# Two feed-forward blocks written as unrolled programs of units across group borders, and the store of the output by group

## What is computed

```
h = jax.nn.silu(hg) * hu              # hg = w_gate x, hu = w_up x, 16 experts
ye = einsum('bsei,edi->bsed', h, w_down)
y = einsum('bsed,bse->bsd', ye, combine) + silu(g) * u @ shared_down_w.T
```

## Time and profile before

| what | us |
|---|---|
| median of 3 runs (lowest to highest) | 5502.06 (5499.12 to 5502.11) |
| profiled execution, its time | 5501.84 |
| its span, first to last instruction | 5500.1 |
| busy in the span: PE / DVE / ACT / POOL | 4484.7 / 3591.8 / 2738.8 / 2465.6 |
| mean granted clock of TensorE, as a share of full speed | 0.897 |

### The profile page before, as it was taken

The page is one execution under the profiler, slowest core; times in us unless marked ns, Lnnn a source line. Parts: engine busy times, 40 slices in busy tenths (PEclk is TensorE's granted clock), DMA queues, the critical chain, the costliest instruction groups (busy, mean ns, idle before and its releaser), DMA issues. The chain is left out here.

```text
span 5500.1 us, 116174 instructions
## 1 busy us (share of the span) xinstructions
PE 4484.7 (82%) x45623; PEld 2775.8 (50%) x45624; DVE 3591.8 (65%) x6873; ACT 2738.8 (50%) x4638; POOL 2465.6 (45%) x2282
## 2 busy tenths in 40 slices
PE   7768999999999999678647888877887689967577
PEld 5545666666666666336523334343563444424344
DVE  4347777777777776475286999999553436547355
ACT  3325666666666666553225656655553235533121
POOL 8436666666666665250275666666332210001100
PEclk7789999999999999788668999999998779977788
DMA  1001111111111111000000000000000000020000
GB/s 23 16 29 28 45 37 29 49 33 45 36 43 37 29 37 29 5 0 3 12 1 14 0 1 1 0 1 1 15 1 0 13 9 16 1 70 5 20 1 8
DMA packets 110396, 102.35 MB, mean 19 GB/s; under 512 B 37095, under 2 KB 80375, under 8 KB 109111
## 3 DMA queue, kind: packets, MB, share of 16 engines
q1 hardware_dynamic: 107831, 94.14, 6.9%
q0 software_dynamic: 2048, 1.05, 0.1%
HBM read 40.18 MB, written 1.18 MB: 8 GB/s over the span
## 5 line engine op out<-in xcount | busy, mean ns | idle before, releaser
L4201 POOL TENSOR_TENSOR l_attn_read<-l_attn_state,l_attn_c_rows 128x1024 f32<-128x1024 f32 x256 | 604.4, 2362 | 291.6 <-DVE l_attn_state L4103 174.4
L2999 POOL TENSOR_TENSOR l_ffn_t<-l_ffn_t 128x512 f32<-128x512 f32 x384 | 487.3, 1269 | 506.5 <-DVE l_ffn_t L2866 506.5
L2597 PE MATMUL psum<-l_ffn_wq,l_ffn_xsT 128*128 128x512 f32 x1152 | 599.6, 612 | 99.3 <-DVE l_ffn_t L2866 97.8
L3823 PE MATMUL psum<-l_attn_read,ident 128*128 128x512 f32 x1024 | 489.9, 596 | 7.3 <-DVE l_attn_yz L4111 5.0
L3005 POOL TENSOR_TENSOR l_ffn_t<-l_ffn_t,l_ffn_ss 128x512 f32<-128x512 f32 x384 | 400.5, 1043 | 0.7 <-DVE l_ffn_ss L2881 0.7
L2862 DVE TENSOR_TENSOR l_ffn_t<-psum,l_ffn_tab 128x512 f32<-128x512 f32 x384 | 258.8, 674 | 121.3 <-ACT l_ffn_sq L2748 118.6
L4103 DVE TENSOR_TENSOR_SCAN l_attn_state<-l_attn_decay,psum 128x1024 f32<-128x1024 f32 x144 | 329.0, 2285 | 4.5
L2645 PEld LDWEIGHTS psum<-l_ffn_pT,l_ffn_v 64*64 64x64 f32 x3072 | 248.8, 135 | 142.9 <-issue 138.8
L2597 PEld LDWEIGHTS psum<-l_ffn_wq,l_ffn_xsT 128*128 128x128 f32 x1152 | 179.4, 191 | 274.0 <-DVE l_ffn_t L2866 237.9
L3979 ACT ACTIVATE l_attn_decay<-l_attn_dt,l_attn_a 128x1016 f32<-128x1016 f32 x256 | 292.9, 1144 | 37.2 <-DVE l_attn_state L4100 33.8
L2645 PE MATMUL psum<-l_ffn_pT,l_ffn_v 64*64 64x64 f32 (+1 forms) x3072 | 306.1, 227 | 1.2 <-ACT l_ffn_pT L2764 1.2
(11 more groups left out here) (908 smaller groups left out, 11415.5 us busy)
## 6 DMA issues: line engine op xcount, KB each, us to landing
l_ffn_vx<-l_ffn_v SPq DMA_DIRECT2D x192, 128.0 KB
l_ffn_vx<-l_ffn_v SPq DMA_DIRECT2D x384, 64.0 KB
l_ffn_wq<-in_L_ffn_Wqkv SPq DMA_DIRECT2D x6, 1536.0 KB, 6.3
l_xattn_toep<-s4d_taps SPq DMA_DIRECT2D x4, 2048.0 KB, 17.1
l_ffn_wo<-in_L_ffn_Wo SPq DMA_DIRECT2D x6, 512.0 KB, 4.1
l_ffn_w<-in_L_ffn_W SPq DMA_DIRECT2D x6, 341.0 KB
l_ffn_w<-in_L_ffn_w SPq DMA_DIRECT2D x3, 512.0 KB, 4.1
x_all<-in_x SPq DMA_DIRECT2D x4, 256.0 KB, 4.2
```

The source lines that it names most:

```text
L2597: nc.tensor.matmul(ring[it % 2], xsT[:, n % 2, m % G, :], w, start=True, stop=True).then_inc(itemed, 1)
L2999: nc.gpsimd.tensor_tensor(t1[:, m % G, i, :], t1[:, m % G, i, :], t2[:, x % 3, :], ALU.add).then_inc(added, 1)
L3823: last = nc.tensor.matmul(total[:, h * GT:(h + 1) * GT], K.ident[:], read[:, k % 3, h * GT:(h + 1) * GT], start=(n == 0), stop=(n == N - 1 ...
L4201: nc.gpsimd.tensor_tensor(read[:, k % 3, :].rearrange("p (h n) -> p h n", h=2), state[:, k % 3, :].rearrange("p (h n) -> p h n", h=2), row ...
```

## The change

Both blocks lose the device loop and the stages in it. Each is one stage with one unrolled program per engine over all NU units: in L2 a group is 2 shared units (a half of the shared expert each) and 8 experts, 40 units in all; in L3 one shared unit and 16 experts, 68 in all. In step s PE does `first(s)` and the later parts of the units s - 1 and s - 2, also where these belong to the group before. What prepares the next group (transposes of x, router, Exp or Tanh, routing steps) stands at fixed steps in the middle of a group; `sc`, `sel`, `total` and `xT` are doubled for it. x is transposed from `x_all` directly. The shared unit's addition starts `total` from x_all (the residual). The norm is `moments` on DVE (four bn_stats, four bn_aggr) behind the last addition of a group, then root and scaling on POOL, which writes x_all: in L2 POOL does it behind the scaling for expert 2 of the next group, in L3 it has nothing else. In L3, SP issues the three loads (sd first) and, when a group is normed, the store of that group, all inside the stage; the final store stage is gone. The matmuls, their shapes and their number are the same; a shared unit of L2 adds its half with its own DVE addition in place of accumulation in PSUM, and ACT's copy of the shared output is gone.

The parts of L2 that set the order (PE, ACT, DVE; `shared(n)` is true for the first two units of a group):

```diff
-        with nc.Fori(0, NB // G) as i:
-            b0 = i * G
-            load_group(K, b0)
...
+            def wait_x3_free(eng, n):
+                if shared(n):
+                    eng.wait_ge(product, n + 1)
+                else:
+                    eng.wait_ge(x3_ready, experts_to(n))
...
+                def first(n):
+                    if n >= 1:
+                        pe.wait_ge(h_ready, n)
+                        wait_x3_free(pe, n - 1)
...
+                    nc.tensor.matmul(H, by_h, src, start=True, stop=True).then_inc(h_dot, 1)
+                    nc.tensor.matmul(X3, by_x3, src, start=True, stop=True).then_inc(x3_dot, 1)
...
+                turn_x(0)
+                route(0)
+                for s in range(NU + 2):
+                    if s + 1 < NU and not shared(s + 1):
+                        turn(s + 1)
+                    if s < NU:
+                        first(s)
+                    if 1 <= s <= NU and not shared(s - 1):
+                        second(s - 1)
+                    if s >= 2:
+                        turn_back(s - 2)
+                    if s < NU and s % PER == 4 and group(s) + 1 < NG:
+                        turn_x(group(s) + 1)
+                    if s < NU and s % PER == 5 and group(s) + 1 < NG:
+                        route(group(s) + 1)
...
+                for s in range(NU):
+                    if s + 1 < NU and not shared(s + 1):
+                        move(s + 1)
+                    silu(s)
+                    if not shared(s):
+                        move_x3(s)
+                    if s % PER == 4 and group(s) + 1 < NG:
+                        move_x(group(s) + 1)
+                    if s % PER == 7 and group(s) + 1 < NG:
+                        exp(group(s) + 1)
...
+                for s in range(1, NU + 2):
+                    if s <= NU:
+                        multiply(s - 1)
+                    if s >= 2:
+                        add(s - 2)
+                        if (s - 2) % PER == PER - 1:
+                            moments(group(s - 2))
+                    if s < NU and s % PER == 6 and group(s) + 1 < NG:
+                        begin_route(group(s) + 1)
+                    if s < NU and s % PER == 8 and group(s) + 1 < NG:
+                        end_route(group(s) + 1)
```

`multiply(n)` waits for turn_back(n - 2) and, of a shared unit, for its Silu and X3; it writes `pr[n % 2]`. `add(n)` waits for turn_back(n). Of L3:

```diff
-        load(K, *[(w[i][:], I[pre + n].rearrange("e a b -> a e b")) for i, n in ((1, "w_up"), (2, "w_down"))], (sd[:], I[pre + "shared_down_w"]))
...
+            @block.sync
+            def _(sp):
+                sp.dma_start(sd[:], I[pre + "shared_down_w"]).then_inc(down_in, 16)
+                sp.dma_start(w[1][:], I[pre + "w_up"].rearrange("e a b -> a e b")).then_inc(up_in, 16)
+                sp.dma_start(w[2][:], I[pre + "w_down"].rearrange("e a b -> a e b")).then_inc(down_in, 16)
+                for g in range(NG):
+                    sp.wait_ge(normed, G * (g + 1))
+                    sp.dma_start(K.out[g * G:(g + 1) * G].rearrange("b t d -> t b d"), K.x_all[:, g * G:(g + 1) * G, :]).then_inc(written, 16)
+                sp.wait_ge(written, 16 * NG)
...
+                for s in range(NU + 2):
+                    if s < NU:
+                        first(s)
+                    if s >= 2:
+                        second(s - 2)
+                    if s < NU and s % PER == 5 and group(s) + 1 < NG:
+                        turn_x(group(s) + 1)
+                    if s < NU and s % PER == 7 and group(s) + 1 < NG:
+                        route(group(s) + 1)
...
+                for s in range(NU + 2):
+                    if s < NU:
+                        multiply(s)
+                    if s >= 2:
+                        add(s - 2)
+                        if (s - 2) % PER == PER - 1:
+                            moments(group(s - 2))
+                    if s < NU and 8 <= s % PER < 13 and group(s) + 1 < NG:
+                        route(group(s) + 1, s % PER - 8)
...
-                sp.dma_start(out.rearrange("b t d -> t b d"), K.x_all[:]).then_inc(stored, 16)
-                sp.wait_ge(stored, 16)
```

More of the change, by code:

```diff
@@ L4548, in l2_ffn @@
 def l2_ffn(K):
-    nc, I = K.nc, K.ins
-    E = 8
-    pre = "L2_ffn_"
+    nc = K.nc
+    E, SH = 8, 2
+    PER = SH + E
+    NU = NG * PER
     with ExitStack() as es:
@@ L4557, in l2_ffn @@
         gate, w, b, sw1, sw2, sw3 = ready.gate, ready.w, ready.b, ready.sw1, ready.sw2, ready.sw3
[L4558 removed]
+        sc, sel = sb("sc", [128, 2, G, E]), sb("sel", [128, 2, G, E])
         m8 = sb("m8", [128, G, 8])
         sm = sb("sm", [128, G])
[L4561 to L4708 removed]
@@ new lines, in l2_ffn @@
+        xs, xsT, hT, x3, pr, xT = (sb(n, [128, 2, GT]) for n in ("xs", "xsT", "hT", "x3", "pr", "xT2"))
+        total = sb("total", [128, 2, G, D])
+        st, mv, rs = sb("st", [128, G, 6]), sb("mv", [128, G, 2]), sb("rs", [128, G])
+        TURN, H, X3, X2, BACK, MISC = (K.bank[0], K.bank[1]), K.bank[2], K.bank[3], K.bank[4], (K.bank[5], K.bank[6]), K.bank[7]
+        group = lambda n: n // PER
+        shared = lambda n: n % PER < SH
+        expert = lambda n: n % PER - SH
+        nth = lambda n: group(n) * E + expert(n)
@@ L4711, in l3_ffn @@
 def l3_ffn(K):
     nc, I = K.nc, K.ins
-    E, TOP = 16, 8
+    E = 16
+    PER = 1 + E
+    NU = NG * PER
     ROUTE = 2.826
@@ L4721, in l3_ffn @@
         sd = sb("sd", [128, D])
-        sc, ch, rp = (sb(n, [128, G, E]) for n in ("sc", "ch", "rp"))
+        sc, ch, rp = sb("sc", [128, 2, G, E]), sb("ch", [128, G, E]), sb("rp", [128, G, E])
         m8 = sb("m8", [128, G, 8])
         sm = sb("sm", [128, G])
-        hT, pr = (sb(n, [128, 2, GT]) for n in ("hT", "pr"))
-        total = sb("total", [128, G, D])
-        load(K, *[(w[i][:], I[pre + n].rearrange("e a b -> a e b")) for i, n in ((1, "w_up"), (2, "w_down"))], (sd[:], I[pre + "shared_down_w"]))
@@ new lines, in l3_ffn @@
+        hT, pr, xT = (sb(n, [128, 2, GT]) for n in ("hT", "pr", "xT2"))
+        total = sb("total", [128, 2, G, D])
+        st, mv, rs = sb("st", [128, G, 6]), sb("mv", [128, G, 2]), sb("rs", [128, G])
+        HG, HU, Y, MISC, LOGIT = K.bank[0:2], K.bank[2:4], K.bank[4:6], K.bank[6], K.bank[7]
+        group = lambda n: n // PER
+        shared = lambda n: n % PER == 0
+        expert = lambda n: n % PER - 1
+        adds_to = lambda n: sum(1 if shared(m) else G for m in range(n + 1))
+        names = ("up_in", "down_in", "x_turned", "x_moved", "logits", "tanhed", "route_step", "g_dot", "u_dot", "silued", "product", "y_dot", "added",
+                 "stats_step", "var_ready", "rstd_step", "rstd_ready", "normed", "written")
@@ L5418, in program @@
             run(l3_ffn)
-        with stage(nc, "stored") as (block, stored):
-            @block.sync
-            def _(sp):
-                sp.dma_start(out.rearrange("b t d -> t b d"), K.x_all[:]).then_inc(stored, 16)
-                sp.wait_ge(stored, 16)
 def kernel(**inputs):
```

436 lines of the change are left out of this document (300 added, 136 removed).

## The result

The changed kernel takes 5373.04 us (median of 4 runs, 5369.75 to 5376.34), the kernel before 5502.09 on the same chip (5499.12 to 5508.3): ratio 0.9767, interval 0.9756 to 0.9778. It is faster by 2.3%, 129 us; the forecast said 138.

The account below looks back on a forecast made before the run. No engine was full, PE fullest; much of each group lay outside the expert pace, with PE mostly idle or at half speed. 5501.84 less 55.2 (layer 2) and 83.2 (layer 3) gave 5364 us; 8 in 10 within 5345 to 5388.

Parts of the forecast that it names:

- its own case: Whole kernel: the forecast without the rivals, 5364 us within 5350 to 5378, chance 0.76.
- The border: Layer 2's group borders: PE waits 2.0 and 3.5 us for shared units' products, the second behind the moments on DVE.
- The clock: Layer 2's three borders: half speed behind the waits loses between nothing and 2.1 us each; 2.1 taken.
- The table switch: Layer 2, next group's preparation: ACT loads tables for Exp and back for Silu, 1.28 us each; PE waits 1.0 us.
- rival 3: ACT: a table switch costs more than its load, 12.6 us more in all, 5376 us; chance 0.04.
- The norm: Each block's end: POOL's norm 0.24 + 1.04 + 1.74, with gaps 3.4 us; layer 2's three earlier norms cost nothing.
- The store: Layer 3's end: issue and landing of the last 256 KB take 4.3 us; the other stores lie under the work.
- Layer 3's slack: DVE in layer 3: product comes 1.9 us before PE needs it, largest backlog 1.2, so nothing on the path.
- Borders at no cost: Layer 2's borders: clock stays up and DVE's order does not hold PE, 26 us less, 5338 us; chance 0.08.
- rival 2: Both blocks: latency holds the pace below PE's, 16 us in layer 2, 6 to 12 in layer 3, 5380 to 5392; chance 0.10.
- the supply of instructions: PE's stream in both blocks: unrolled programs not supplied fast enough, 48 ns on each of 2912 instructions, 5502 or more; chance 0.02.
- The rest: Everything outside the two feed-forward blocks and the final store: taken as fixed, 5501.84 us less some 516.

Follow-up runs that it names:

- the changed kernel's third trace: The changed kernel as it is, run once more in more rounds: 5366.76 us (median of 5 runs), ratio 0.9764 to the kernel before.
- layer 2 alone: The kernel before with only the new `l2_ffn`: 5450.14 us, ratio 0.9906 to the kernel before.
- the run with X2: The changed kernel with the second shared unit's x3 of each layer-2 group put into the X2 bank: 5353.25 us, ratio 0.9734.
- The kernel with the norm in pieces: Changed kernel plus x3 in X2, both blocks' last norm scaling on DVE, layer 2's norm split on POOL's queue: 5343.55 us, ratio 0.9715 to the kernel before.

## Why the prediction was right, and where it was off

The forecast was 5364 us in 5345 to 5388, its own case 5350 to 5378, and 5373.04 was measured: the likeliest case held. The borders, the paces and the idle-free layer 3 came as forecast. That the two blocks came within 2.7 us of their sum is in part luck, for errors of both signs cancel in it: the norm was put 1.3 too short at either end, the clock 2.9 and the store 2.1 too long. By its own steps, for the profiled execution (in layer 2, t from 4129.25, which is 2.0 us behind the end of l2_xattn, as the forecast set it):

| step | forecast | measured |
|---|---|---|
| L2, start to end of step 3 | 17.6 | 17.8 (to 4147.09) |
| rest of group 0 | 22.6 | 22.5 (to 4169.55) |
| a whole border group, with its fall of the clock | 42.6 | 42.0 |
| last group | 40.3 | 38.2 |
| last adds, moments | 6.5 | 6.5 |
| norm on POOL | 3.4 | 4.7 |
| end of the stage | 1.9 | 1.8 |
| L3, start to end of step 2 | 11.6 | 11.5 (5174.43 to 5185.93) |
| steps, preparation, last adds | 178.2 | 178.1 (to 5364.06) |
| moments, norm | 5.1 | 6.4 |
| store, end of the stage | 6.0 | 3.9 |

**The border.** The mechanism held at each of three: two waits, both ended by a shared unit's product, bn_stats ahead of the second, and none in layer 3. Sizes: 1.70 and 3.13 us for 2.0 and 3.5. Moving the moments took 1.7 us off the second wait and nothing off the first, and the second bank took away both.

**The clock.** Taken as 2.1 at each of three borders; it fell at two in the profiled execution and cost 1.7 each. The code does not decide the third: in the changed kernel's third trace and in that of layer 2 alone the clock fell there too, stayed at 0.50 for 6.8 us and cost 3.0. In both, the clock had come back 0.9 us later at the block's start than in the traces without a third fall (10.8 us behind the end of l2_xattn for 9.9), which cost another 0.4. The two go together in all five traces of this block; that one brings the other is not shown.

**The table switch.** The wait was 0.67 us, taken as 1.0. Each of the two loads is 1.28, and the next instruction starts 0.01 to 0.02 us behind it:

```profile
4161.79 1.28 ACT L4700 ACT_TABLE_LOAD   x1
4163.08 0.23 ACT L4700 ACTIVATE l_ffn_sc<-l_ffn_sc 128x32 f32<-128x32 f32 x1
...
4163.80 1.28 ACT L4716 ACT_TABLE_LOAD   x1
4165.10 0.69 ACT L4716 ACTIVATE l_ffn_hT<-psum,l_ffn_b 128x512 f32<-128x512 f32 x1
```

So rival 3 fell. The Trainium skill (ScalarE: Activation LUTs, What ACT_TABLE_LOAD costs) has 1.38 us more for a drain at each switch; this trace has none of it, neither behind the loads nor ahead of them.

**The norm.** The step that failed in size is the 1.74 us for POOL's four operations, read off l2_xattn's norm. The same shape here takes 3.13:

```profile
4299.73 3.13 POOL L4605 TENSOR_SCALAR x_all<-l_ffn_total,l_ffn_mv,l_ffn_rs 128x128 f32<-128x128 f32 x4
...
5367.33 3.14 POOL L5017 TENSOR_SCALAR x_all<-l_ffn_total,l_ffn_mv,l_ffn_rs 128x128 f32<-128x128 f32 x4
```

l2_xattn multiplies by rs and adds a prepared nb, L4605 subtracts the mean and multiplies by the root. The mis-sizing cost 1.3 us at each block's end, and it stood in the three inner norms as well: that they cost nothing, by 5.5 us of slack, was true only because the border waits had lengthened the way. In the run with X2, without them, POOL held PE for 2.17 us at each border.

**The store.** 2.3 us from issue to landing, taken as 4.2 from a load; with the end of the stage 2.1 us less than forecast.

**Layer 3's slack.** A largest backlog of 1.2 against 1.9 of slack: nothing on the path, and that held with margin; the slack measured is 2.6 us. SP's new order, with sd first, cost nothing: steps 0 to 2 ended where they were put.

**The other rivals.** Borders at no cost (5338) was false for this kernel. The kernel with the norm in pieces, where they were made so, came near (5343.55), but some 4 us of its gain are the two ends' norms on DVE. The pace: steps are 3.45 and 2.61 us as before; so the latencies of rival 2 did not show, and the supply of instructions cost nothing in the 170 us in which PE was never idle.

**The rest.** Taking the rest as fixed is where the sum missed its own execution. The blocks gave 2.7 us more than forecast and the rest took 15.4, so that this execution (5376.34) lies 13 us above its sum, and the median (5373.04) 5 below the top of the forecast's own case; a little more, and that case would have been missed with every step of the blocks right. Of the 15.4, most belong to that one execution, since the same program again had a rest 13 and 16 us shorter, and 6.0 of them are half-speed time that a trace of the kernel before shows at the same place; whether some 4 to 8 us on average belong to the program stays open. No run moved the code of the blocks without changing what it does, which would tell.

## What to carry to other kernels

When a loop is unrolled over its group borders, what is left is the order written on each queue: look at each border for a single bank whose reader stands behind other work, and for a helper engine's lump ahead of an input that is wanted soon. Cutting that lump into pieces of one step each brought 9.0 us in the block, nearly what the second bank did (9.7). Price the next wait before counting the whole of the one removed: of 14.5 us of waits, 6.5 came back at the next queue. A sum of good block prices still carries what the untouched code varies by, here 23 us between the lowest and the highest trace, and the range has to hold it.

## What the runs showed of the hardware that was not expected

Four 128x128 operations of POOL with two per-partition operands took 3.13 us as subtract and multiply, and 1.74 as multiply and add in l2_xattn; DVE took 1.11 for the former. The granted clock fell or stayed up at the same border of the same program in different executions (third border of the changed kernel: up in two, down in one). A half-speed stretch lasted 3.4 us at the first two borders and 6.8 at the third. A wait of 1.7 and one of 3.13 us with 2.6 us between brought it at the first two borders in all three; 1.71 and 1.43 never did in the one trace that had them, and a single wait of 2.2 us brought it at one border of three, in both traces that had it. Far from the change, a stretch with the same 192 matmuls took 23.0 or 29.0 us, in both kernels.
